# Two transformer blocks on one core: restacking the first heads by products, identity products in waits, and a new order table

## The reference, cut to what matters

```
ada = silu(c) @ W_ada + b_ada; shift, scale, gate for attention and mlp
h = layernorm(x) * (1 + scale) + shift
q, k, v = h @ W_qkv + b_qkv          # layer 0 with bias, layer 1 without
w = softmax(q k^T / sqrt(9))         # layer 1: causal mask
x = x + gate * ((w v) @ W_proj + b_proj)
h = layernorm(x) * (1 + scale) + shift
x = x + gate * (act(h @ W1 + b1) @ W2 + b2)   # gelu(tanh) in layer 0, silu in layer 1
```

## Time and profile before

| | us |
|---|---|
| median of the runs | 337.88 |
| profiled execution, its own time | 339.11 |
| its span | 337.4 |
| TensorE busy | 287.9 |
| VectorE busy | 237.5 |
| ScalarE busy | 176.5 |
| GpSimd busy | 91.9 |

### The profile page before, as it was taken

The page is one execution under the profiler, slowest core; times in us unless marked ns, Lnnn a source line. Parts: engine busy times, 40 slices in busy tenths (PEclk is TensorE's granted clock), DMA queues, the critical chain, the costliest instruction groups (busy, mean ns, idle before and its releaser), DMA issues.

```text
span 337.4 us, 5548 instructions
## 1 busy us (share of the span) xinstructions
PE 287.9 (85%) x1727; PEld 133.8 (40%) x1727; DVE 237.5 (70%) x708; ACT 176.5 (52%) x379; POOL 91.9 (27%) x199
## 2 busy tenths in 40 slices
PE   2570899999889999999999878998989998898696
PEld 2340563534222252363343432833323443346365
DVE  4653688799998879688734898399997868431552
ACT  2120003267688658967785119276745767682240
POOL 4400017510122181111205222233433544411100
PEclk9996555599999999999999859799996999999879
DMA  7115680005530000000156100003650000001001
GB/s 225 45 35 153 180 222 1 0 2 158 162 108 1 3 1 1 2 1 1 41 167 185 33 1 1 3 0 84 182 162 3 4 1 4 1 2 35 0 2 35
DMA packets 21772, 18.99 MB, mean 56 GB/s; under 512 B 2934, under 2 KB 21213, under 8 KB 21744
## 3 DMA queue, kind: packets, MB, share of 16 engines
q1 hardware_dynamic: 20014, 17.90, 18.3%
q10 hardware_dynamic: 706, 0.55, 0.6%
q0 software_dynamic: 1024, 0.20, 0.3%
HBM read 10.67 MB, written 7.67 MB: 54 GB/s over the span
## 4 chain that ended last, share of the span: by engine, by line
PE 63%; DVE 13%; ACT 8%; issue 6%; DMA 5%; SPq 3%; POOL 1%; POOLq 0%; ACTq 0%; DVEq 0%
PE OB L1190 12%; PE PB L1147 8%; PE PB L1236 7%; PE PB L1170 6%; PE PB L1224 6%; ACT probs L842 5%; DVE PB L1024 4%; DMA QS<-mT 3%; PE PB L1128 3%; PE PB L1118 2%; PE PB L1216 2%; SPq L648 2%; PE PB L1197 2%; PE PB L1215 2%; PE PB L1225 2%
## 5 line engine op out<-in xcount | busy, mean ns | idle before, releaser
L842 ACT ACTIVATE probs<-PB 128x512 f32<-128x512 f32 (+3 forms) x256 | 115.4, 523 | 60.8 <-PE PB L1170 52.2
L1027 DVE TENSOR_REDUCE top<-PB 128x1 f32<-128x512 f32 x128 | 79.4, 683 | 12.9 <-PE PB L1147 12.4
L1147 PE MATMUL PB<-KS,QS 54*128 54x512 bf16 (+3 forms) x256 | 65.2, 392 | 16.4 <-DMA KS<-qk_parts 11.5
L1170 PE MATMUL PB<-QS,KS 57*128 57x512 bf16 (+3 forms) x256 | 61.4, 357 | 5.8 <-ACT probs L842 3.0
L1024 DVE CUSTOM_DVE_ANT_0 PB<-PB,mask_qk 128x128 f32<-128x128 f32 (+3 forms) x128 | 59.1, 521 | 9.8 <-PE PB L1147 9.5
L1190 PE MATMUL OB<-probs,V 128*10 128x512 f32 (+3 forms) x512 | 58.3, 529 | 0.7 <-POOL probs L765 0.3
L1147 PEld LDWEIGHTS PB<-KS,QS 54*128 54x128 bf16 x256 | 16.7, 98 | 57.0 <-issue 32.9
L1170 PEld LDWEIGHTS PB<-QS,KS 57*128 57x128 bf16 x256 | 16.6, 95 | 47.4 <-issue 22.0
L765 POOL TENSOR_SCALAR_AFFINE_SELECT probs<-probs 128x512 f32<-128x512 f32 x32 | 20.7, 648 | 49.0 <-ACT probs L842 48.9
L788 POOL DMA_DIRECT2D QS<-mT x32 | 18.6, 583 | 36.4 <-ACT mT L832 36.3
L778 POOL CAST msp<-top 128x16 bf16<-128x16 f32 x16 | 3.9, 246 | 86.0 <-DVE top L1027 66.7
(11 more groups left out here) (119 smaller groups left out, 377.8 us busy)
## 6 DMA issues: line engine op xcount, KB each, us to landing
qk_parts<-parts SPq DMA_DIRECT2D x8, 189.0 KB
QS<-qk_parts SPq DMA_DIRECT2D x12, 108.0 KB
KS<-qk_parts SPq DMA_DIRECT2D x12, 108.0 KB
QS<-qk_parts SPq DMA_DIRECT2D x8, 162.0 KB
KS<-qk_parts SPq DMA_DIRECT2D x8, 162.0 KB
qk_parts<-parts SPq DMA_DIRECT2D x8, 135.0 KB, 2.5
qk_parts<-parts SPq DMA_DIRECT2D x8, 126.0 KB
qk_parts<-parts SPq DMA_DIRECT2D x8, 108.0 KB
```

The source lines that it names most:

```text
L842: nc.scalar.activation(probs[:, kt % 2, j, q0:T], bank_of(item)[:, q0:T], ACT.Exp, scale=SCALE).then_inc(bank_free[BANK[item]], 1)
L1027: ins = nc.vector.tensor_reduce(m, bank[:, 0:w], AX.X, ALU.max)
L1147: ins = nc.tensor.matmul(bank[:, 0:w], QS[b][rows, i, qt * P:(qt + 1) * P], KS[b][rows, i, 0:w], start=True, stop=True)
L1170: ins = nc.tensor.matmul(bank[:, q0:T], KS[b][rows, i, kt * P:(kt + 1) * P], QS[b][rows, i, q0:T], start=True, stop=True)
```

## The change

Three groups of edits, all in one file.

1. The first chunk (heads 0 to 3) of three of the four (layer, batch) pairs, `SELECTED`, is stacked without DRAM. TensorE multiplies the parts, which lie on partitions, with a 0/1 matrix `sel`, and the PSUM bank that comes out is copied into QS (by ScalarE) or KS (by VectorE). The second and third chunk now have six heads each. The mid part is made by ScalarE, the low part by POOL except for the first chunk. The strips are filled with zero rows: 61 rows for the maxima and 64 for the scores, where there were 54 and 57.
2. Identity products (`FILL`) are put ahead of items for which the planner finds TensorE waiting while few of its rows are in use. There are 79 in 46 places: 12 before the first stacking product (7 of them before the first item), 12 in the tail.
3. The order: `HASTE` has a value for each group and kind of item, `fc2` and `acol` are split in two items, products of another kind after a strip product are charged `TURN`, the remainder `hr` moves from VectorE to POOL except for three, and the first three `acol` that stood in the first groups move to the weights stream.

```
-CHUNKS = [(0, 4), (4, 11), (11, H)]
+CHUNKS = [(0, 4), (4, 10), (10, H)]
+SROW = STRIP - 3
+SELECTED = [(0, 0), (1, 0), (1, 1)]
+SEL = [(i, w) for i in range(HG // 2) for w in range(2)]
+ON_DVE = [("hr", 0, 0, 0, 0), ("hr", 1, 1, 1, 1), ("hr", 1, 1, 1, 2)]
+def splitter(c):
+    return "POOL" if c else "DVE"
+TURN = 90
+FILLER, MOST = 218, 8
-HOLD = {"attend": 5, "max": 4, "shift": 1}
-OTHERS, CALM = 2, 3
+HOLD = {"attend": 3, "max": 3, "shift": 5}
+OTHERS, CALM = 3, 5
+HASTE = {
+    "max": (-464000, -464000, 73000, 87000, -1000, -113000, -677000, -232000, 372000, -9000, -9000, -37000, 9000, -383000, 61000, 0),
...
+            if k is not None and start > free["PE"]:
+                begin = max(free["PE"], left_at[k] + HANDOVER if holder[k][0] else 0)
...
+                fillers[item] = max(0, min(MOST, wanted, int((start - begin) // (FILLER * pace))))
...
+                for _ in range(FILL.get(item, 0)):
+                    nc.tensor.matmul(bank[:, 0:P], ident[:, :], ident[:, :], start=True, stop=True)
...
+                elif kind == "sel":
+                    l, b, i, w = args
+                    pe.wait_ge(sel_ready, 1)
+                    pe.wait_ge(high_ready, QKN["qk", l, b, 0])
+                    nc.tensor.matmul(bank, sel[:, w, i, 0, :], parts[0:ONE + 1, 0, 0, :], start=True, stop=False)
+                    pe.wait_ge(mid_ready, MID["mid", l, b, 0])
+                    nc.tensor.matmul(bank, sel[:, w, i, 1, :], parts[0:ONE + 1, 0, 1, :], start=False, stop=False)
+                elif kind == "selb":
+                    l, b, i, w = args
+                    pe.wait_ge(low_ready[0], LOW["low", l, b, 0])
+                    nc.tensor.matmul(bank, sel[:, w, i, 2, :], parts[0:ONE + 1, 0, 2, :], start=False, stop=True).then_inc(filled_bank, 1)
...
-                    rows, i = strip(h + j, MROW), (h + j) // 2
+                    rows, i = strip(h + j, SROW), (h + j) // 2
...
-                    rows, i = strip(h + j, KROWS), (h + j) // 2
+                    rows, i = strip(h + j, STRIP), (h + j) // 2
...
-            sp.dma_start(cond[:, 0, :], a["cond_1152"][0:P]).then_inc(cond_in, 16)
-            sp.dma_start(cond_r[0:R, 0, :], a["cond_1152"][P:C]).then_inc(cond_in, 16)
...
+            pool.dma_start(cond[:, 0, :], a["cond_1152"][0:P]).then_inc(cond_in, 16)
+            pool.dma_start(cond_r[0:R, 0, :], a["cond_1152"][P:C]).then_inc(cond_in, 16)
```

More of the change, by code:

```diff
@@ L234, in steps @@
             w = keys_of(l, t)
-            add("max", "PE", ("max", g, u), w / 2.4 + 10, *(("DMA", ("rows", l, b, c)) for c in chunks_of(g)))
+            add("max", "PE", ("max", g, u), w / 2.4 + 10, *(("DMA", ("rows", l, b, c)) for c in chunks_of(g) if c or (l, b) not in SELECTED),
+                *((("DVE" if x[1] else "ACT"), ("sel", l, b, *x)) for x in SEL if g % NG == 0 and (l, b) in SELECTED))
             add("max", "DVE", ("max", g, u), w * 1.04 + (118 if l else 108), ("PE", ("max", g, u)),
@@ L360, in plan @@
                     start = max(start, t + HANDOVER if holder[k][0] else 0)
+                if engine == "PE" and half and item[0] not in ("max", "scores"):
+                    start += TURN
                 mine_best.append((start, -urgency[engine, item] - haste(stream, item), engine, stream, item, k))
@@ L537, in two_block_kernel @@
         QKN = ordinals(("qk",))
+        MID = ordinals(("mid",))
         GATE = ordinals(("gate",))
         GELU_U = {i: n for n, i in enumerate((i for i in SIDE if i[0] == "fc1" and i[1] == 0), 1)}
+        LOW = {i: n for late in range(2) for n, i in enumerate((i for i in SIDE if i[0] == "low" and (i[3] > 0) == late), 1)}
         def full(eng, item):
@@ L584, in two_block_kernel, with stores, store_parts, load_rows @@
         ada = [("L0_cond_W_ada", "L0_cond_b_ada"), ("L1_cond_Wa", "L1_cond_ba")]
+        def stores(l, b, c):
+            return sum(1 for n in range(l * B + b + 1) if c or (n // B, n % B) not in SELECTED)
+        def store_parts(eng, l, b, c):
+            eng.wait_ge(low_ready[c > 0], LOW["low", l, b, c])
+            n = width(c) // 2
+            runs = (((0, 3, 1, 0), (0, 2, 1, 3), (0, 1, 1, 5)), ((0, 1, 3, 0), (1, 1, 2, 3), (2, 1, 1, 5)))
+            for w in range(2):
+                for s, many, times, slot in runs[w]:
+                    src = parts[w * n:(w + 1) * n, c, s:s + many, :]
+                    if times > 1:
+                        src = src.to_broadcast([n, times, T])
+                    dst = scratch[l][b][c][w, slot:slot + many * times].rearrange("s d h t -> (d h) s t")
+                    eng.dma_start(dst, src).then_inc(parts_out[c], 16)
+        def load_rows(eng, l, b, c):
+            if l and c == 1:
+                full(eng, ("scores", (b + 1) * NG - 1, LAST))
+            eng.wait_ge(parts_out[c], 6 * 16 * stores(l, b, c))
+            h0, h1 = CHUNKS[c]
+            for q in range(2):
+                first = h0 + (h0 + q) % 2
+                rows, many = slice(STRIP * q, STRIP * q + MROW), len(range(first, h1, 2))
+                for w in range(2):
+                    src = scratch[l][b][c][w].rearrange("s d h t -> (s d) h t")[:, first - h0:h1 - h0:2, :]
+                    eng.dma_start((QS, KS)[w][b][rows, first // 2:first // 2 + many, :], src).then_inc(stacked[l * B + b][c], 16)
         @block.sync
```

358 lines of the change are left out of this document (238 added, 120 removed).

## The result

The changed kernel takes 327.19 us (median of 4 runs, 326.55 to 327.92); the kernel before took 337.88 beside it (3 runs, 337.73 to 341.08). The ratio is 0.9655 with a 95% interval of 0.9584 to 0.9727: 3.5% faster. 305 us were forecast, and 290 to 324 as the range. The direction was right; of the 33 us of the sum 13 came, measured on the spans of the two profiled executions. The profiled execution took 326.55 us, its span is 324.8.

What follows compares the result with a forecast made beforehand. The prediction saw no one bound, with the largest losses in S1 with S2, and S4. Its terms, -8.4 - 9.5 - 3 - 20 + 10 - 2 = -32.9, took 337.4 to 304.5, plus 0.5: 305 us, range 290 to 324.

Steps and rivals of the forecast that it cites:

- S1: Start to VectorE's first row maximum, 35.9 us before; restacking by products was to bring it to 27.5, -8.4 (24 to 31).
- S2: From the first maximum to group 0's last transpose, 46.6 us before; forecast 37, -9.5, with TensorE keeping up.
- The rival in which the level stays low: Clock stays low in S2 and recurs in S4 and S5; S2 +4, about 321 us in all; chance 0.17.
- S3: From group 0's to group 7's transpose, 102.4 us before; forecast -3, bounds -12 and +6.
- its hole of 8 us on VectorE closes: In S3: VectorE's gap closes because group 8's maxima no longer wait for a landing; all of it gives bound -12.
- S4: Between the layers, group 7's to group 8's transpose, 47.6 us before; new order was to give 27, -20 (-24 to -8).
- cost nothing where TensorE really waits: The 55 identity products between the early ones and the tail: free in true waits, 14.3 us at most, 2 taken.
- S5: From group 8's to group 15's transpose, 77.5 us before; work moved in from S4, forecast +10 (+4 to +18).
- of a stage that had 25 us of room: In S5: VectorE's 52.4 us of work becomes some 68 within the stage's room; part of the +10.
- the gain of S4 is given back in S5: Rival: the work only changes its stage; S4 gives -8, S5 +16, 323 us in all; chance 0.13.
- S6: Serial tail after group 15's transpose, 27.4 us before; identity products holding the clock give -2 (-3 to +2).
- The rule weighed: Skill's rule: recent busyness sets the clock, so identity products help only in true waits and S2's low stretch ends itself.

Runs made afterwards that it cites:

- e10: The changed kernel with none of its 79 identity products, all else the same: 327.06 us, ratio 0.964 to the kernel before.
- e2: The changed kernel without the 28 identity products of the first 63 us: 330.28 us, ratio 0.9711 to the kernel before.
- e7: e1 with the three column products, their evictions and a gate moved back among the maxima of groups 0 and 1: 340.01 us, ratio 0.9998.
- e8: The changed kernel with the old order and column product places, no identity products; restacking, new splits and zero rows kept: 354.03 us, ratio 1.0442.
- e4: The kernel before with 44 identity products ahead of its first maximum, nothing else changed: 339.63 us, ratio 1.0004.
- e1: The changed kernel without its 39 identity products between group 0's transpose and the tail: 323.43 us, ratio 0.9542 to the kernel before.
- e9: The changed kernel without the 12 identity products between the transposes of groups 3 and 8: 323.91 us, ratio 0.9562 to the kernel before.
- e3: The changed kernel with 54 instead of 61 rows in the strips of the maxima: 330.66 us, ratio 0.9771 to the kernel before.
- e6: The changed kernel with 24 more identity products in S5, in groups 9 to 14: 336.05 us, ratio 0.9897 to the kernel before.

## Why the prediction was right or wrong

**S1, right.** First maximum at 25.73, inside 24 to 31. Part of its size was not foreseen: the remainder `hr`, 12.40 to 15.54 in the earlier trace rows, now takes 11.84 to 12.92 (rows in the last section). By e10, up to 2.0 us of the 10.2 come from the identity products. The same product shows how, first in the change, then in e10, where it comes again for the next chunk (line numbers one higher):

```profile
16.32 1.02 PE L1315 MATMUL PB<-hT,w_qk 128*108 128x512 f32 x2
```
```profile
17.37 1.91 PE L1316 MATMUL PB<-hT,w_qk 128*108 128x512 f32 x2
...
22.99 1.02 PE L1316 MATMUL PB<-hT,w_qk 128*108 128x512 f32 x2
```

1.91 us is the price at the low level and 1.02 at the full one, so in e10 the full clock came later, although the clock column has 1.00 for S1 of both: for the first microseconds of a profile the durations are the better witness. The effect varies from run to run: with the early identity products the profiled first maximum lay between 25.7 and 27.0 us in seven kernels, without them at 27.2 (e2) and 27.7 (e10). The prediction's own terms, 22.3 + 5 - 1, give 26.3 and not the 27.5 that it wrote; the length of the first remainder was no term of it, so that the measured 25.73 lies so near is in part luck.

**S2, right in size and cause.** Group 0 is finished at 63.3 (60 to 69 forecast), the full clock is back at 35.9. e7 shows the cause directly: the column products, put back, cost 18.9 us, half of it their own time. e8 agrees. The rival in which the level stays low (0.17) did not come, but its condition is real: e4 and e7 are kernels in which it holds. The forecast spoke of 4 us for it; with the column products in place S2 takes 57.0 (e7) and 58.7 us (e8) instead of 37.6.

**S3, wrong: the step "its hole of 8 us on VectorE closes".** The hole did close: in the ten us that answer to it VectorE now works 7.87 us instead of 1.83 (row 156.90:166.90 above). The stage grew all the same. A hole on VectorE is time only if TensorE has one too, and the row I quoted says that it had none: TensorE worked 9.72 of those 10.00 us. VectorE's idle time over the stage did not fall either, 23.6 us before and 25.3 after. TensorE had 6.6 us of idle time left in S3; its busy time rose by 11.0, from 95.76 to 106.74, and the stage by 6.1. End to end the column products take 5.3 us, stacking 2.8, identity products 1.5; the maxima give 1.9 back, and the rest 1.3. Measured +6.1 is the upper bound of that step, "all that arrives". I had both terms and chose between the bounds by the wrong engine. How much of each arrival was paid is less sure: e7 takes the column products away and gets at most 3.1 of their 5.3 us back, e1 takes the identity products away and S3 is no shorter (109.8), and the other terms were not tried one by one.

A second misreading lies in the same sum: the two remainders that leave VectorE were put at "3.1 us each". That is the price of the first one alone. The others cost 1.1 us in the kernel before (rows in the last section), so VectorE was relieved of less than the text says.

**S4, mostly right.** First scores of layer 1 at 179.11, 7.3 us after group 7's transpose (under 10 forecast), and the stage is under 32. Of the miss of 3.6 us the 11 identity products in it explain all: they take 5.7 us end to end, and without them (or all but one, in e9) the stage has 27.3, 26.8 and 27.6 us (e10, e1, e9), where 27 was forecast. That they "cost nothing where TensorE really waits" stood in the text with its bound of 14.3 us; what failed is the belief in the plan's waits.

**S5, wrong in size: "of a stage that had 25 us of room".** The room was VectorE's; TensorE, at 71.3 of 77.5 us, had 6.2. Without identity products (e10) VectorE's work rose from 52.4 to 64.0, less than the 68 forecast; TensorE's from 71.3 to 86.7, more than the 80 forecast (83 less 3.4); and the stage by 17.0, much as TensorE's 15.4 and not as VectorE's 11.6. What moved in is, end to end, `fc2` 4.2, stacking 3.6, `qk` 3.4, transposes 2.6, `mT` 2.0 and maxima 1.0. The forecast names `fc2` for TensorE and the maxima; the "norm and split" of batch 1 it names as 6 us of VectorE's only, but their transposes and products are TensorE's, and stacking in S5 it does not name.

**S4 and S5 together** make the point: 125.1 us before, 126.5 after, 121.8 in e10. A stage cut by a mark shows work that changes sides as a gain. So the rival "the gain of S4 is given back in S5" (0.13) is what happened, with other sizes: -16.4 and +17.8 where it had -8 and +16. From S3 to S5 TensorE's busy time is 208.0 of 227.5 us before and 217.8 of 231.7 in e10: 9.8 us of work more on an engine that had 19.5 left over. Part of its waits took it up and part did not: the three stages together grew by 4.2 us.

**S6.** -0.9 of -2. The low level is gone as forecast (the window of 20.40 us above has clock 1.00), and e10 shows the identity products as the cause: without them the stage has clock 0.82 and 1.9 us more. In its place the stage took over `fc2` work, 52 instructions and 6.4 us end to end instead of 40 and 4.9.

**The rule weighed.** In e4 the clock falls at 37.5 us and stays low for 30.70 us, of which TensorE counts as busy for 30.21; the kernel before has the same. e3 points the same way more weakly: it runs the same instructions with the same durations (382 and 389 ns), was 3.5 us slower by the medians, and in the profiled pair over half of the difference lies where e1, with all its rows, has it too. The Trainium skill, "TensorE: Matmul & The Clock Gate", section "What's actually happening", sets the level by how busy the engine has recently been. By that rule the low stretches of e4 and of the kernel before would have ended early; the traces do not agree. Which property of the column products, or of what stands around them, keeps the level low, no run here isolates. The prediction's sentence "add no column, so no time" on the zero rows is right for one product; what the rows do to the clock stays open.

**The range.** 290 to 324 was too narrow above. The upper bounds of S3 and S5 alone (+6, +18) give 305 + 9 + 8 = 322, and the identity products of S4 most of the rest. Both bounds were met together; that they share one cause, TensorE's load, is my reading of the two stages. I had treated them as independent.

## What to carry to other kernels

Before idle time of one engine is booked as gain, read the busy time of the others in the same window: in S5, where TensorE was busy for 92.05 of 95.30 us, 24 small products more cost 8.7 us (e6). Keep thin products out of the first maxima: three sets of column products there cost 18.9 us, where at the end of S2 and in S3 they took some 8 (e7). Sum the moved work over both sides of a mark before a shorter stage is called a gain. Filler products belong only in waits that a trace of the new order shows, not in those that a plan expects: leaving 12 of 79 out gave 323.9 us, and leaving out all 39 late ones 323.4, the best kernels of this study and not to be told apart.

## What the runs showed of the hardware

**Neighbours on GpSimd.** Two of the five operations of the remainder on 128x64 elements, on VectorE in the kernel before: the first remainder, beside work on GpSimd, and then the second, with no work on GpSimd beside these rows:

```profile
12.40 0.59 DVE L982 TENSOR_TENSOR hy<-hn,modr 128x64 f32<-128x64 f32 x1
13.72 1.41 DVE L987 CAST hs<-hy 128x64 fp32r<-128x64 f32 x1
...
12.24 1.36 POOL L702 CAST w_fc_s<-raw_f 17x576 fp32r<-17x576 f32 x2
13.68 1.39 POOL L704 TENSOR_TENSOR w_fc_s<-raw_f,w_fc_s 17x576 fp32r<-17x576 f32 x1
```
```profile
68.04 0.22 DVE L982 TENSOR_TENSOR hy<-hn,modr 128x64 f32<-128x64 f32 x1
...
68.55 0.20 DVE L987 CAST hs<-hy 128x64 fp32r<-128x64 f32 x1
```

The five take 3.1 us the first time and 1.1 us, from 68.04 to 69.12, the second. The remainders of 64 columns that follow in the kernel before have casts of 0.20 us too, and so has the first one of the changed kernel, where GpSimd is idle at that time. The cast of 1.41 us begins 0.04 us after the GpSimd operation of 1.39 us and ends within 0.1 us of its end. So the same instruction of the same kernel is seven times slower beside it; no run moves the GpSimd operation alone.

**The price of a filler.** An identity product in float32 was put at 0.26 us. 44 in a row take 10.03 us at full clock, 0.23 each (e4). Between other products one costs 0.4 (e6), and 0.72 to 0.79 at 1.2 GHz (rows under e9).

**Zero rows.** Seven rows of zeros per strip change no duration (382 and 389 ns). The kernel without them was 3.5 us slower by the medians, at a mean clock of 0.948 to 0.953 instead of 0.963 to 0.968 (e3); how much of this is due to them stays open.

**GpSimd's low part** on 108x512 elements takes 1.156 us. VectorE's `rest` has the same shape, though it reads PSUM and writes float32, and takes 0.683:

```profile
L873 POOL TENSOR_TENSOR parts<-rest,parts 108x512 bf16<-108x512 f32 x8 | 9.2, 1156 | 33.7 <-ACT parts L993 33.7
```
```profile
L1172 DVE TENSOR_TENSOR rest<-PB,parts 108x512 f32<-108x512 f32 x8 | 5.5, 683 | 1.0 <-ACT parts L988 1.0
```
